# Gated cross-attention with routed experts: part of the second layer's weights split inside the expert stage, fewer and other weight pieces before it, four sizes of rows

## What is computed

```python
# attention, per batch and head (S = 512, D = 256, 8 heads of 32)
log_D = cumulative forget gates + input gate, masked to s >= t
C = (q @ k.T / sqrt(32)) * exp(log_D - max)
h = (C / (max(|C.sum()|, exp(-max)) + eps)) @ v
x = x + tanh(g_xattn) * layernorm(h) * ln_scale
# experts
scores = sigmoid(layernorm(x) @ gate.T + bias)        # 4096 tokens x 9
top 2 per token, weights cw normalised to sum 1
for e in range(9):
    hdn = silu(xn @ w1[e].T) * (xn @ w3[e].T)         # 256 -> 704
    out = out + cw[:, e] * (hdn @ w2[e].T)            # 704 -> 256
x = x + tanh(g_ffn) * out
```

## Time and profile before

| | us |
|---|---|
| median of 3 runs | 740.82 |
| lowest and highest of them | 740.18 and 741.02 |
| the profiled execution's own time | 739.6 |
| its span (first to last instruction) | 737.7 |
| PE busy in the span | 645.8 (88%) |
| POOL, DVE, ACT busy | 401.9, 510.8, 383.1 |
| read from and written to device memory | 153.82 MB and 38.18 MB |

### The profile page before, as it was taken

How to read it: one execution, slowest core, us unless ns; L and a number is a source line. 1 busy time by engine, 2 the same in 40 slices (tenths; PEclk the granted TensorE clock), 3 DMA queues, 4 the chain that set the end, 5 groups by cost and what they waited for, 6 DMA issues and landing times.

```text
span 737.7 us, 19870 instructions
## 1 busy us (share of the span) xinstructions
PE 645.8 (88%) x7020; PEld 525.3 (71%) x7020; DVE 510.8 (69%) x1393; ACT 383.1 (52%) x995; POOL 401.9 (54%) x417
## 2 busy tenths in 40 slices
PE   4928699879999972489999999999999999999993
PEld 2414467567677762358898988889888898889892
DVE  8666998999888888926565665656656565566652
ACT  4566777878778850624443444434434343443431
POOL 2056999989999950043444445352553544443432
PEclk9965655585555555579999999999999999999998
DMA  9737898978899723956898989989899898989962
GB/s 311 282 100 253 257 310 283 285 266 267 273 304 302 255 106 24 332 168 205 251 352 260 345 287 277 322 268 328 268 315 336 247 358 250 317 307 276 322 162 21
DMA packets 88483, 192.75 MB, mean 261 GB/s; under 512 B 14593, under 2 KB 48258, under 8 KB 88386
## 3 DMA queue, kind: packets, MB, share of 16 engines
q1 hardware_dynamic: 66421, 153.47, 62.3%
q0 software_dynamic: 13216, 17.94, 12.5%
q10 hardware_dynamic: 8749, 20.09, 7.0%
HBM read 153.82 MB, written 38.18 MB: 260 GB/s over the span
## 4 chain that ended last, share of the span: by engine, by line
PE 68%; DVE 11%; POOL 8%; issue 6%; ACT 2%; DMA 2%; SPq 1%; ACTq 0%; DVEq 0%; POOLq 0%
PE bank L1171 50%; POOL whl L526 4%; PE bank L1165 2%; PE bank L801 2%; DVE Cl L644 2%; PE bank L327 2%; PE bank L558 2%; PE bank L560 2%; PE bank L536 1%; PE bank L1217 1%; POOL x L767 1%; PE bank L570 1%; DVE R L1041 1%; PE bank L789 1%; POOL vp L609 1%
## 5 line engine op out<-in xcount | busy, mean ns | idle before, releaser
L1171 PE MATMUL bank<-xh,w 128*128 128x256 bf16 (+2 forms) x2024 | 259.7, 246 | 2.9 <-issue 1.3
L1171 PE MATMUL bank<-xl,w 128*128 128x256 bf16 (+2 forms) x1012 | 218.6, 246 | 3.1 <-issue 3.1
L1153 POOL DMA_INDIRECT out<-res,TS x73 | 116.1, 1590 | 153.7 <-DMA out<-res,TS 85.7
L1274 ACT ACTIVATE sg<-bank 128x256 f32<-128x256 f32 (+2 forms) x236 | 83.4, 353 | 218.8 <-PE bank L1171 210.1
L1171 PEld LDWEIGHTS bank<-xh,w 128*128 128x128 bf16 x2024 | 169.0, 99 | 20.3 <-issue 5.2
L1324 DVE TENSOR_TENSOR hf<-sg,bank 128x256 f32<-128x256 f32 (+1 forms) x180 | 69.7, 387 | 95.9 <-ACT sg L1274 91.6
L1143 POOL DMA_INDIRECT xg<-y_d,TG x73 | 71.8, 983 | 100.9 <-DVE cwt L1240 56.5
L1171 PE MATMUL bank<-w,hh 128*128 128x256 bf16 x756 | 122.9, 273 | 2.2 <-DVE hh L1291 2.2
L526 POOL TENSOR_TENSOR whl<-wst,whl 128x408 bf16<-128x408 f32 x96 | 95.7, 1023 | 41.4 <-ACT whl L511 40.0
L1171 PEld LDWEIGHTS bank<-xl,w 128*128 128x128 bf16 x1012 | 97.7, 99 | 10.5 <-issue 3.4
L1262 ACT CAST hh<-hf 128x256 bf16<-128x256 f32 (+1 forms) x216 | 80.3, 372 | 11.1 <-DVE hf L1326 10.5
(11 more groups left out here) (217 smaller groups left out, 1102.3 us busy)
## 6 DMA issues: line engine op xcount, KB each, us to landing
w<-w_d SPq DMA_DIRECT2D x46, 1408.0 KB
w<-w_d SPq DMA_DIRECT2D x46, 768.0 KB
wst<-in_wts SPq DMA_DIRECT2D x32, 612.0 KB, 6.0
w_d<-whl ACTq DMA_DIRECT2D x32, 612.0 KB, 7.3
vb<-in_kv SPq DMA_DIRECT2D x8, 528.0 KB, 5.7
xa<-in_x SPq DMA_DIRECT2D x8, 512.0 KB, 7.3
kT<-in_kv SPq DMA_DIRECT2D x8, 512.0 KB, 8.2
xc<-in_x SPq DMA_DIRECT2D x8, 512.0 KB, 7.8
```

Of the source, the lines that this page charges most:

```text
L1153: nc.gpsimd.indirect_dma_start(out, bass.IndirectOffsetOnAxis(ap=TS[a:z, c:c + 1], axis=0), res[s % 3][a:z, j, :], None, bounds_check=TOK ...
L1171: mm = nc.tensor.matmul(dst, l, r, start=(n == 0), stop=(n == len(pairs) - 1))
L1274: nc.scalar.activation(sg[n % 2][0:K, 0:W], bank[0:K, 2 + n % 4, 0:W], ACT.Silu).then_inc(f_sg, 1)
```

## The change

- The array of the expert weights loses the first four of the six column blocks of the second layer: `HB = 4`, `HW = 1024` columns per expert. They stand in a second input `whot`, in float32. The remaining `wts` has 29952 columns, cut in 24 pieces of 1248 (`NPC`) instead of 32 of 1224. The table `PIECE` leaves out the slots with t % 10 in (2, 5, 8) and ends with slot 27.
- In the expert stage `f_w2_sync` loads, per set, two column blocks in both parts from `w_d` (256 KB) and 1024 float32 columns from `whot` into `wf` (512 KB, two buffers). ACT casts them (`f_w2_act`) and DVE subtracts (`f_w2_dve`), and layer 2 waits for that (`f_w2l`).
- Sets have four sizes, 512, 256, 128 and 64 rows, with 9, 9, 9 and 10 sets. A set of 512 rows is worked in two slots of 256 on the same weights. There are 37 sets instead of 46, and still 46 slots with the same numbers of rows in the same order. The routing gets a fourth size: its tables grow from 3 to 4 levels.
- Ahead of the slots: POOL makes piece 1 after DVE's last gate instruction (`g_dve` 14 instead of 10) and piece 2 right after it; PE makes the first scores ahead of the turning of the gates; ACT casts the last `mx` tile earlier, and piece 3's high part ahead of `Ch` in slot -1; SP loads piece 3 ahead of the `EB` tiles.

```diff
-WE = W13 + W2C
+HB = 4
+HW = HB * D
+WC = W2C - HW
+WE = W13 + WC
-WCH = WALL // NT
+NPC = 24
+WCH = WALL // NPC
-SIZE = (256, 128, 64)
-CAP = (27, 9, 10)
+SIZE = (512, 256, 128, 64)
+CAP = (9, 9, 9, 10)
...
         def g_pe_all(pe):
+            pe.wait_ge(b_uz, 1)
+            b_s_pe(pe, 0)
             pe.wait_ge(g_act, 7)
...
-            if t not in (13, 29, 30, 31) and len(PIECE) + NAHEAD < NT:
+            if t % 10 not in (2, 5, 8) and len(PIECE) + NAHEAD < NPC:
...
+            V.memset(stride[:, 0:1], float(WE)).then_inc(r_str, 1)
+            V.memset(stride[:, 1:2], float(HW)).then_inc(r_str, 1)
...
-        SEQ = [(2, 0)]
-        for i in range(CAP[1]):
-            full, half, quarter = [(0, 3 * i + k) for k in range(3)], (1, i), (2, i + 1)
-            SEQ += full + [half, quarter] if i < CAP[1] - 1 else full[:2] + [half, quarter] + full[2:]
+        SEQ = [(3, 0)] + [(l, i + (l == 3)) for i in range(CAP[0]) for l in ((0, 1, 2, 3) if i < CAP[0] - 1 else (0, 2, 3, 1))]
...
         def f_w2_sync(sp, n):
...
-            sp.dma_start(w2_[n % W3][:, :, :], w_d[:, :, bass.ds(e + W13, W2C)]).then_inc(f_w2[n % W3], 16)
+            sp.dma_start(w2_[n % W3][:, :, HW:], w_d[:, :, bass.ds(e + W13, WC)]).then_inc(f_w2[n % W3], 16)
+            f = sp.value_load(eoff[0:1, 1, KIND[n]:KIND[n] + 1], min_val=0, max_val=(NE - 1) * HW)
+            ge(sp, f_w2l, n - 1)
+            sp.dma_start(wf[n % 2][:, :], whot[:, bass.ds(f, HW)]).then_inc(f_wf[n % 2], 16)
+
+        def f_w2_act(act, n):
+            ge(act, f_wf[n % 2], n // 2 * 16 + 16)
+            if n >= W3:
+                ge(act, f_y, last[n - W3] + 1)
+            nc.scalar.copy(w2_[n % W3][:, 0, 0:HW], wf[n % 2][:, :]).then_inc(f_w2h, 1)
+
+        def f_w2_dve(dve, n):
+            ge(dve, f_w2h, n + 1)
+            nc.vector.tensor_tensor(w2_[n % W3][:, 1, 0:HW], wf[n % 2][:, :], w2_[n % W3][:, 0, 0:HW], ALU.subtract).then_inc(f_w2l, 1)
...
             ge(pe, f_w2[sl.set % W3], (sl.set // W3) * 16 + 16)
+            ge(pe, f_w2l, sl.set + 1)
...
+                if head[s]:
+                    f_w2_act(act, SL[s].set)
                 f_h_act(act, s)
...
+                if head[s] and s == NS - 1:
+                    f_w2_dve(dve, SL[s].set)
                 f_h_dve(dve, s)
+                if head[s] and s < NS - 1:
+                    f_w2_dve(dve, SL[s].set)
...
-            pool.wait_ge(g_dve, 10)
+            pool.wait_ge(g_dve, 14)
             w_pool(pool, 1)
+            w_pool(pool, 2)
             b_v_pool(pool, 0)
             pool.wait_ge(g_cols, 2)
             b_kw_pool(pool, 0)
-            w_pool(pool, 2)
```

More of the change, by code:

```diff
@@ L63, with build @@
 NEG = -1e30
-def build(nc, x, kv, wgate, fib, lnrow, gsc, wroute, rbias, wts, out):
+def build(nc, x, kv, wgate, fib, lnrow, gsc, wroute, rbias, wts, whot, out):
     with ExitStack() as ctx:
@@ L888, in slot_sync @@
                 c_sync(sp, b + 1)
-            if t in PIECE and PIECE[t] + 1 < NT:
+            if t in PIECE and PIECE[t] + 1 < NPC:
                 w_sync(sp, PIECE[t] + 1)
@@ L1110, in build @@
         w2_ = [sb(f"w2_{w}", [P, 2, W2C], BF16) for w in range(W3)]
+        wf = [sb(f"wf{w}", [P, HW]) for w in range(2)]
         xg = [sb(f"xg{w}", [P, 2, YW]) for w in range(3)]
@@ L1125, in build @@
         KIND = {sl.set: sl.kind for sl in SL}
+        head = [s == 0 or SL[s].set != SL[s - 1].set for s in range(NS)]
         def f_w1_sync(sp, n):
-            e = sp.value_load(eoff[0:1, KIND[n]:KIND[n] + 1], min_val=0, max_val=(NE - 1) * WE)
+            e = sp.value_load(eoff[0:1, 0, KIND[n]:KIND[n] + 1], min_val=0, max_val=(NE - 1) * WE)
             if n >= W3:
@@ L1384, in _ @@
             g_e_sync(sp)
+            w_sync(sp, 3)
             b_e_sync(sp, 0)
-            for n in range(3, NAHEAD + 2):
-                w_sync(sp, n)
+            w_sync(sp, 4)
             for t in range(NT + 4):
@@ L1421, in _ @@
             b_vh_act(act, 0)
-            mx_act(act, 2 * HG - 1)
             w_store(act, 1)
```

34 lines of the change are left out of this document (19 added, 15 removed).

## The result

| | before | after |
|---|---|---|
| median, us (4 runs each, same chip) | 740.56 | 761.56 |
| lowest and highest, us | 740.18 and 741.02 | 758.02 and 763.81 |
| ratio to before, 95% interval | | 1.0269 (1.0242 to 1.0297) |
| the profiled execution's own time, us | 739.6 | 760.75 |
| its span, us | 737.7 | 758.6 |

The changed kernel is 2.7% slower, where 737.0 us had been forecast. The experiments add a second number, which turned out to be as important: on three other chips the kernel before takes 731 us and not 740, and on the two of them on which the changed kernel was run it is only 0.3% slower. Executions more than 1.5% above the fastest of their kernel (one of 1450.8 us of the kernel before and one of 1179.5 us of idle_sub_third are the extreme ones) are left out of every ratio.

The account below looks back on a forecast made before the run. PE was taken to bound the expert stage, PE and POOL to tie in the attention. Terms -4.3 - 1.0 - 2.5 + 1.3 + 1.2 + 1.5 = -3.8 take 740.8 to 737.0 us; range 730.5 to 744.

Parts of the forecast that it names:

- What bounds the kernel: Whole kernel: PE limits the expert stage, with only 5.4 us idle to win; PE and POOL tie in the attention.
- Expert stage, the new wait (+1.5): Expert stage: ACT's cast waits for the float32 columns; 1.5 us slower for eight tight places together, bounds zero and 10.
- The late load: Rival, expert stage: float32 columns land over 0.7 us later than put, PE stalls, 10 us lost, about 746; chance 0.14.
- Expert stage, later slots: Expert stage after its start: the weight subtraction on DVE and ACT's cast are hidden, DVE going from 61% to 73%.
- Expert stage, start (+1.2): Start of the expert stage: subtraction of set 1's weights stands ahead of `xl`, which PE awaits; 1.2 us slower.
- The start (-4.3): Attention up to chunk 1: 4.3 us faster, 1.0 for the gates and 3.3 from piece 3 landing near 61 to 62.
- the start doesn't shorten: Rival: piece 3's load lands at 64 as before, only 1 of 4.3 us comes; chance 0.23 together with the slots failing.
- The gates: Start of the attention: piece 1 waits for DVE's gate instructions, so the last gate exponential comes 1.4 earlier; 1.0 us counted.
- Slots 1 to 4 (-1.0): Early attention slots: one weight piece less, so POOL's freed time is worth 1.0 us.
- Slots 5 to 31 (-2.5): Rest of the attention: 16 pieces instead of 23, 2.5 us faster; best end 9.5 us faster, worst 5 us slower.
- Routing (+1.3): Routing: DVE's chain grows with the fourth level, 1.3 us slower, all on the path.
- the clock rises: Rival, attention: PE waits less for POOL and gets full clock more often, giving 727.5 us; chance 0.11.

Follow-up runs that it names:

- idle_sub_third: Kernel before with the four sizes alone, plus a DVE subtraction of two constants ahead of `cwt`, result unused; 1.0037 of before on chip 4.
- changed_again: The changed kernel as it is, run again on chip 3; 1.0035 of before.
- phase_64: Changed kernel with 64 more one-column products on PE ahead of the first expert slot; 751.46 us, 1.0156 of before on chip 1.
- scatter_first: Changed kernel with POOL issuing the scatter of slot s - 6 ahead of the gather of slot s; 1.0097 of before on chip 2.
- cast_back: Changed kernel with DVE's subtraction behind `cwt` and `xl`, and ACT's cast of piece 3 back behind `Ch`; 726.82 us, 0.9946 of before on chip 4.

## Why the prediction was wrong

**What bounds the kernel** was read rightly for the stages. But "nothing but 5.4 us of idle time" in the expert stage was taken as a fact of the kernel, and I never asked what that time was. The 6% of "issue" in the earlier trace rows would not have told me by itself, since 29 of its 43 us lie in the attention and 9 from 320 us on. On chips 2 to 4 most of the idle time does not exist: a period of five slots takes 43.3 us there and 44.1 in the kernel before on the chip of the result.

**Expert stage, the new wait (+1.5).** As a price of its own right: in changed_again four of the periods are 0.2 to 0.4 us longer than 43.33, 1.2 us in all, and ACT does wait for `wf` (up to 4.0 us at a time) with PE hardly behind it. The late load as a loss of 10 us did not happen in this kernel; how near it is, its neighbours show, in which PE waits 5.9 us in all for `hf` (phase_64, scatter_first). The wait of 1.46 us at 734.39, once, for the last set's subtracted weights was not foreseen.

**Expert stage, later slots: the step that failed.** "There the same subtraction and ACT's cast are hidden: DVE goes from 61% to 73%." Hidden from PE's data they were. I followed the waits for DVE's results as far as PE and did not follow `cwt` to POOL, whose gathers and scatters it times. I costed the subtraction by who waits for it, and not by who waits for what stands behind it on DVE. This step carries nearly the whole miss of 24.6 us: with it undone the kernel is at 0.9976 of before (chip 5), where the forecast stood at 0.995, and with nothing but such an operation added to the kernel with the four sizes it is at 1.0259.

**Expert stage, start (+1.2).** The wait came as forecast, 2.39 instead of 1.25 us on chip 3 and 2.30 instead of 1.16 on the chip of the result; that it can take the clock with it, another 1.7 and 1.5 us, was not foreseen.

**The start (-4.3).** Failed: chunk 1 came 2.1 us later instead of 4.3 earlier. The step "so it lands near 61 to 62" was wrong, a landing worked out from the issue: in the thirteen kernels with this start ACT's cast came at 62.9 to 65.8. And ACT's place in front of `Ch` was seen as a risk for chunk 1 only, not for chunk 0 behind it on DVE. This is my rival *the start doesn't shorten*, and worse than I had it. The gates did give time (L434's successor takes 0.67 us instead of 1.43), but PE then waited 2.08 us for the mask load.

**Slots 1 to 4 (-1.0)** gave 0.3: 25.14 us from chunk 1 to 5 against 25.45. **Slots 5 to 31 (-2.5)** gave 3.9: 166.6 against 170.5. The mechanism was right, a removed piece helps where PE has slack, and the size somewhat small. **Routing (+1.3)** was right: 1.2. The granted clock in the attention stayed at 0.58 of full from 98 to 265 us in both kernels, so the rival *the clock rises* did not come.

With both failed steps mended the sum comes near its old value. cast_back, against the clock hand of the kernel before: chunk 1 at 71.39 instead of 72.90 (-1.5), chunk 5 2.6 us earlier (another -1.1), slots 5 to 31 in 166.7 us instead of 170.5 (-3.8), routing +1.2 and waits for `wf` +1.2 is -4.0 us; measured were -3.8, the forecast's own number. That is luck in part. It belongs to another kernel than the one that I had in front of me, and the rows compared are from two chips: beside idle_sub_third, which has the start and the pieces of before and ran on chip 4 too, cast_back has chunk 1 3.0 us and chunk 31 8.1 us earlier.

## What to carry to other kernels

- An operation put on an engine with spare time is only free if everything behind it in that queue is free to move too. Follow the queue, not only the result: what does the next instruction release, on which engine, and on what does that come to lie?
- When a share of the chain is "issue", ask for it by stage and find its rows before forecasting. A stage with such places is sensitive to shifts of a microsecond, and on another chip it may behave otherwise.
- A cast or copy that waits for a transfer belongs behind the work that can already run; the landing follows from what is in flight, not from the time of issue.
